# Placing the first pair's offset convolution and one weight product differently in TensorE's queue

## The reference, cut to what matters

```python
# block 0: x is (4, 256, 16, 16), w1 makes 64 channels
out = relu(group_norm(conv(x, w1), gn1_scale, gn1_bias))   # 32 groups of 2 channels: "pairs"
om = conv(out, w_off, pad=1) + b_off                       # 3x3, 27 channels
off_x, off_y, mask = om[:, :9], om[:, 9:18], sigmoid(om[:, 18:])
sampled = bilinear_sample(out, grid_y + ky + off_y, grid_x + kx + off_x) * mask
out = einsum('bckhw,ock->bohw', sampled, w2)               # 9 taps, 64 -> 64
out = relu(group_norm(out, gn2_scale, gn2_bias))
x = relu(group_norm(conv(out, w3), gn3_scale, gn3_bias) + x)
# block 1: 1x1, depthwise 3x3, 3x3 and 1x1 convolutions on quantised values, then relu(h + residual)
```

## Time and profile before

| | |
|---|---|
| median of 3 runs | 90.74 us (89.81 to 90.78) |
| the profiled execution | 90.92 us, span in the trace 89.1 us |
| TensorE matmul, busy | 74.9 us (84% of the span) |
| TensorE weight loads | 51.4 us (58%) |
| VectorE | 64.8 us (73%) |
| ScalarE | 49.6 us (56%) |
| GpSimd | 5.0 us (6%) |

### The profile page before, as it was taken

One profiled execution on the slowest core, in us unless ns is written; L12 is line 12 of the kernel. 1 busy time (PEld: TensorE's weight loads), 2 busy tenths in 40 slices (PEclk: granted clock), 3 DMA queues, 4 the chain that ended last, 5 costly groups with the idle time before them and its releaser, 6 DMA issues.

```text
span 89.1 us, 2173 instructions
## 1 busy us (share of the span) xinstructions
PE 74.9 (84%) x893; PEld 51.4 (58%) x893; DVE 64.8 (73%) x174; ACT 49.6 (56%) x88; POOL 5.0 (6%) x10
## 2 busy tenths in 40 slices
PE   5986999996899898999999999899579877779600
PEld 1332666474698797889988896355223374555400
DVE  0224539999999789999896725899895784867850
ACT  4203165679974999996868003807562254632660
POOL 7601010000000000000003100000000000000000
PEclk9999999999999999999999999999999999999999
DMA  1999800000000000000000000000000000000076
GB/s 29 328 318 324 329 9 0 0 7 0 0 7 0 0 0 7 4 11 0 0 7 0 0 0 7 0 0 0 0 0 0 0 0 0 0 7 4 0 256 215
DMA packets 3274, 4.17 MB, mean 47 GB/s; under 512 B 256, under 2 KB 2688, under 8 KB 3264
## 3 DMA queue, kind: packets, MB, share of 16 engines
q1 hardware_dynamic: 2992, 3.76, 12.7%
q10 hardware_dynamic: 272, 0.26, 0.9%
HBM read 2.98 MB, written 1.05 MB: 45 GB/s over the span
## 4 chain that ended last, share of the span: by engine, by line
PE 43%; DVE 29%; ACT 12%; DMA 6%; issue 4%; SPq 2%; DVEq 0%; ACTq 0%
PE acc L488 15%; PE slot L475 9%; DVE g_rows L912 9%; DMA x_sb<-x 6%; PE acc L616 4%; DVE g_cols L1014 3%; ACT g_cols L813 3%; PE acc L595 3%; PE slot L403 3%; ACT g_cols L720 2%; PE slot L524 2%; DVE g_cols L1055 2%; ACT pad L777 2%; PE slot L556 2%; DVE unused L1031 2%
## 5 line engine op out<-in xcount | busy, mean ns | idle before, releaser
L912 DVE TENSOR_TENSOR g_rows<-hats 128x2304 f32<-128x2304 f32 (+1 forms) x12 | 20.6, 1752 | 0.1
L720 ACT ACTIVATE g_cols<-slot 128x768 f32<-128x768 f32 x24 | 17.8, 830 | 3.7 <-PE slot L475 3.7
L488 PE MATMUL acc<-g_cols,v_sb 128*64 128x128 f32 x288 | 17.7, 276 | 0.0
L488 PEld LDWEIGHTS acc<-g_cols,v_sb 128*64 128x64 f32 x288 | 15.5, 137 | 1.1 <-issue 0.3
L366 PE MATMUL slot<-zeros 128*128 128x512 bf16 x54 | 14.8, 409 | 1.0 <-DVE zeros L832 1.0
L475 PE MATMUL slot<-consts_sb,g_rows 64*128 64x64 f32 x288 | 11.8, 226 | 2.1 <-DVE g_rows L912 1.7
L475 PEld LDWEIGHTS slot<-consts_sb,g_rows 64*128 64x128 f32 x288 | 10.3, 140 | 3.9 <-DVE g_rows L912 2.7
L366 PEld LDWEIGHTS slot<-zeros 128*128 128x128 bf16 x54 | 5.5, 109 | 6.9 <-issue 2.1
L777 ACT ACTIVATE pad<-g_cols 64x256 bf16<-64x256 int8 x8 | 3.3, 418 | 4.9 <-DVE g_cols L1055 4.8
L843 DVE BATCH_NORM_STATS2 stats<-acc 128x6 f32<-128x256 f32 x4 | 1.7, 431 | 4.3 <-PE acc L378 2.6
L403 PE MATMUL slot<-feat,woff_sb 128*64 128x256 f32 x36 | 4.7, 385 | 0.0
(11 more groups left out here) (137 smaller groups left out, 116.4 us busy)
## 6 DMA issues: line engine op xcount, KB each, us to landing
out<-g_cols SPq DMA_DIRECT2D x4, 256.0 KB, 2.3
x_sb<-x SPq DMA_DIRECT2D x3, 256.0 KB, 4.7
wq_sb<-wq SPq DMA_DIRECT2D x1, 484.5 KB, 6.5
woff_sb<-woff SPq DMA_DIRECT2D x1, 288.0 KB, 5.7
w_sb<-w SPq DMA_DIRECT2D x1, 288.0 KB, 5.8
x_sb<-x ACTq DMA_DIRECT2D x1, 256.0 KB, 3.1
w_sb<-w SPq DMA_DIRECT2D x1, 256.0 KB, 6.5
consts_sb<-consts SPq DMA_DIRECT2D x1, 232.0 KB, 5.7
```

Of the source, the lines that this page charges most:

```text
L488: mm = nc.tensor.matmul(acc[b2][rows(h), at:at + P], v_sb[:, B2 * h + b2, q, k, :], g_cols[t][h][:, NQ * k + q, :], start=(k == 0 and q == ...
L720: nc.scalar.activation(dst.rearrange("p k (r n) -> p k r n", r=HALVES), src.rearrange("p r (k n) -> p k r n", k=per), ACT.Copy).then_inc(g ...
L912: tt(g_rows[i % 3][:, taps], hats[:, t, h, 1, taps].unsqueeze(3).to_broadcast(shape), hats[:, t, h, 0, taps].unsqueeze(2).to_broadcast(sha ...
```

## The change

In TensorE's program the order of the first stage is changed. Before: `conv1(1)`, three idle products, the second pair's sums `pair_sums(2, 1)`, the whole offset convolution of pair 0, that of pair 1 with `om_turn(0)` after its second step, four weight products, `om_turn(1)`. After: `conv1(1)`, two steps of the offset convolution of pair 0, the second pair's sums, the other three steps, weight product 0, then the offset convolution of pair 1 with `om_turn(0)` as before, weight products 1 to 3, `om_turn(1)`. The three idle products are gone. The programs of the other engines and of the queues stay as they are.

```diff
             pair_sums(1, 0)
             conv1(1)
-            idle(IDLE[2], spare)
-            pair_sums(2, 1)
...
-            pe.wait_ge(woff_in, 16)
-            for b2 in range(B2):
-                pe.wait_ge(feat_ready, b2 + 1)
-                for s in range(TAPS_A):
-                    mm = om_step(b2, s)
-                    if b2 == 1 and s == 1:
-                        pe.wait_ge(consts_in, 16)
-                        om_turn(0)
-                mm.then_inc(om_done, 1)
...
-            pe.wait_ge(w2_in, 16)
...
-            for i in range(4):
+            pe.wait_ge(woff_in, 16)
+            pe.wait_ge(feat_ready, 1)
+            for s in range(TAPS_A):
+                mm = om_step(0, s)
+                if s == 1:
+                    pair_sums(2, 1)
+            mm.then_inc(om_done, 1)
+            pe.wait_ge(w2_in, 16)
+            make_v(0)
+            pe.wait_ge(feat_ready, 2)
+            for s in range(TAPS_A):
+                mm = om_step(1, s)
+                if s == 1:
+                    pe.wait_ge(consts_in, 16)
+                    om_turn(0)
+            mm.then_inc(om_done, 1)
+            for i in range(1, 4):
                 make_v(i)
             om_turn(1)
```

## The result

The changed kernel takes 92.10 us (median of 4 runs, 91.50 to 93.22) against 90.76 for the kernel before (4 runs, 89.81 to 92.42). The ratio is 1.0161 with a 95% interval of 1.0109 to 1.0212: slower by 1.4 us (1.0 to 1.9), where 0.7 was forecast. The profiled execution took 92.19 us, with a span of 90.4. In a few executions of nearly every version TensorE's clock falls for a stretch; the ratios here leave out the executions recognised as such, but those of e1 to e4 still hold one or two of them (mean clock 0.973 to 0.975), so there the median of the others is given too.

A forecast was written before the change was run, and what follows sets the result against it. TensorE's row of offset steps and weight products, which sets ScalarE's copies, was taken as the bound. -1.14 + 0.53 + 1.05 + twice 0.14 gave 0.73 us with rounding; against median 90.74, 91.5 us, own range 91.0 to 92.0.

The forecast's parts named there:

- What bounds the kernel: First stage: TensorE's offset steps and weight products set ScalarE's copies; product 4's lateness, 0.73 us, goes through to the end.
- The rival in which the delay is absorbed: Between 25 and 32 us TensorE or ScalarE has slack, so the delay vanishes: 90.7 us; chance 11%.
- The prices: TensorE's first-stage row: offset slot 0.216 us, restart 0.05, switch 0.09, sums 0.53, four weight products 1.92.
- Weight product 0: Ahead of pair 1's convolution: 1.05 us, 0.58 of it not hidden in the wait for features; nothing given back later.
- Idle products out, steps of pair 0 up: TensorE behind `conv1(1)`: the first offset step starts at about 8.88 in place of 10.02, 1.14 us gained.
- Late weights: Rival: `woff` landing over 0.58 us late delays pair 1's steps, 0.1 us per further 0.1; 92.0 for 1 us; chance 4%.
- The clock: Rival: without idle products before the first offset step, TensorE falls to 1.2 GHz, 6.5 us more, 98 us; chance 2%.

The follow-up runs named there:

- e1: The changed kernel run once more with nothing altered; 92.24 us, ratio 1.0203 to the kernel before.
- e4: e2 with the second pair's sums after one step of pair 0 in place of two; 91.19 us, ratio 1.0054 to the kernel before.
- e3: The changed kernel with weight products 0 and 1 both ahead of pair 1's convolution, in other banks; 91.59 us, ratio 1.0122 to the kernel before.
- e6: The kernel before with weight product 0 alone moved between the offset convolutions, the `w2` wait ahead of the first step; 93.49 us, ratio 1.0219 without clock falls.
- e2: The changed kernel with weight product 0 back behind the offset convolutions; 91.56 us, ratio 1.0104 to the kernel before.
- e5: The kernel before with only the three idle products removed; ratio 1.0001 for 6 of 12 executions, median of all 12 91.52 us.
- e10: The changed kernel with its first offset step also waiting for transfer `w2`; median 96.57 us, 93.08 us in the one execution without a clock fall.
- e11: The changed kernel with the three idle products put back behind `conv1(1)`; 92.29 us, ratio 1.0153 to the kernel before.
- e8: The changed kernel with two unused ScalarE copies ahead of pair 0's normalisation; median 93.94 us, ratio 1.0227 for the two executions without clock falls.
- e14: The changed kernel with its first offset step held until `w2` lands, five idle products in the wait; 93.52 us, ratio 1.0281 to the kernel before.

## Why the prediction was right in its mechanism and half the size

- *What bounds the kernel.* Right: TensorE's row up to product 4 sets ScalarE's copies and the end; 1.22 us late at product 4 is 1.22 at the first sampling product and at the end. The rival in which the delay is absorbed is out.
- *The prices.* Right to 0.02 us: slots, restarts, switches, 0.53 for the sums, 1.05 for the product, 5.05 in all where 5.04 was said.
- *Weight product 0.* Right: a lone half-array product takes what a pair takes (e3, e6), and three products take what four took. Its price ahead of pair 1 is 0.59 us in the rows of e1 and e2, and 0.7 to 0.8 in their times; 0.58 was said in the forecast.
- *Idle products out, steps of pair 0 up.* This is the step that failed: "the first step starts at about 8.88 in place of 10.02: 1.14 us gained". Both ends were taken from one execution. The 10.02 rests on a late landing of x; usually the old order starts at about 9.8. The 8.88 rests on "`feat` of pair 0 is earlier", true of the profile of before, of e2 and of e3, and false in the other profiles of the new order; by the spans it is usually about 9.3. The term measured some 0.5 us by the spans and 0.6 by the profiles. So the 92.10 lies outside the forecast's own 91.0 to 92.0. The row of `conv1(0)` and the wait for x were in the profile. Had the gain been left open between 0 and 1.14 us, the sum would have run from 91.5 to 92.6 (an estimate: 90.74 + 1.87 less the gain).
- *Late weights.* This rival has a reading wrong. It lets 0.58 us of lateness of `woff` pass free, until the features of pair 1 and not product 0 set the steps of pair 1. But the first steps, the sums, those features and product 0 all stand behind the same wait, so each 0.1 us costs 0.1 from the start: 92.5 for 1 us by its own sum, not 92.0. No profile has `woff` later than that of before, so it didn't matter here.
- *The clock.* Given 2% as a rival, and for the changed kernel's median it did not decide. But its argument, that the pause for x had left the clock alone, does not carry over to every pause: in e5 a wait of 0.78 us without idle products let the clock fall in about half of the executions. In the changed kernel the wait ahead of the first step is longer, 0.97 us, and its two profiles show no fall there; what tells the two cases apart stays open.

## What to carry to other kernels

A gain made of two moments of one profile, "starts at a in place of b", is only as good as the reason for each moment: for both, look up what comes second-last, and ask whether it moves between executions (a landing, the first products at the start). Work that fills half of the array is best moved in pairs; here a lone half cost as much as a pair where it went (1.05 us) and freed nothing where it came from (three took 1.91 us, four 1.92). In a row that has no waits each cut between shapes costs (here 0.14 us), so a filler pays only where the engine would wait at least as long.

## What the runs showed of the hardware

- TensorE's first products run at half speed for a time that differs between executions. In the profile of before the products of zeros ahead of `conv1(0)` start 0.43 us apart (2.67, 3.10, 3.53), those at 8.67 0.22 apart; the rows show no lower granted clock at the start. The same eight products of `conv1(0)` took from 1.17 (e2) over 1.30, 1.44 and 1.78 to 1.98 us (e4, e5), a wait for x among them, against 1.08 for the eight of `conv1(1)` where they run in one piece.
- Three idle products of 0.22 us each, in a wait, made the difference between a fall to 1.2 GHz in 6 of 12 executions (e5: 4.92 us for instructions that take 3.24) and in 4 of 68. In e10, with 2.1 us of nothing ahead of the first step, it fell in five of six executions.
- The changed kernel and its relatives also lost the clock near 25.4 us in some executions, at a price of 1.43 us on 40 sampling products (e1, e11). In both, TensorE had turned thirds with waits before it, and was busy for 1.03 of 2.00 us between 22 and 24 us in e1. The profiles of e2, e8 and e14 have such a fall too, at some moment between 24.7 and 27.4 us. The windows of e1:

```profile
22.00:24.00 2.00, 1.03 (x26) 0.82 (x24) 1.93 (x4) 2.00 (x5) 0.00 (x0) 1.00 0.00 0
24.00:26.00 2.00, 1.78 (x36) 1.44 (x34) 1.93 (x3) 2.00 (x4) 0.00 (x0) 0.84 0.00 0
26.00:28.00 2.00, 2.00 (x21) 2.00 (x20) 2.00 (x3) 1.08 (x2) 0.00 (x0) 0.50 0.04 8
```

The kernel before has the same thin stretch (busy for 1.04 of 2.00 us between 21 and 23 us). Its mean clock was 0.975 or less in 4 of the 68 runs beside the experiments, that of the changed kernel in 3 of 10. With e2, e3, e4 and e11, which share its early first step, it is 12 of 40. So the new order loses the clock more often, a cost that the ratios above leave out. Why is not settled; putting the idle products back did not help (2 of 6).
